# A state-space and FP4 feed-forward kernel: turned xn of group 0 ahead of x of group 1 in the x bank, small VectorE operands in PSUM, group 1 normalised on GpSimd

## The reference

```python
xn = _layernorm(x, axis=-1)
x = x + attn(xn, ...) + ffn(xn, ...)

# attn: per channel a complex recurrence along the sequence, written in the
# reference as an FFT convolution; then times gate = 1 - exp(-decay * scale), real part
phazor = exp((phazor_angle * 1j - decay) * exp(ln_phazor_scale))
y = conv(xn, phazor ** t * phazor_init) + last_conv * phazor ** (t + 1)

# ffn: every operand is quantised to FP4 (E2M1) in blocks of 16, then dequantised
gate, up = q(xn) @ q(w_gate).T, q(xn) @ q(w_up).T       # 128 -> 352
h = silu(gate) * up
out = q(h) @ q(w_down).T                                # 352 -> 128
# q: scale = max(|block|) / 6, rounds |value / scale| to 0, 0.5, 1, 1.5, 2, 3, 4, 6, times scale
```

## Time and profile before

| | us |
|---|---|
| median of 3 runs | 121.84 |
| lowest, highest | 121.81, 121.91 |
| profiled execution, whole | 121.87 |
| its span in the profile | 119.9 |
| busy in it: TensorE | 112.0 |
| VectorE | 102.8 |
| ScalarE | 100.9 |
| GpSimd | 99.7 |

### The profile page before, as it was taken

How to read it: one execution, slowest core, us unless ns; L and a number is a source line. 1 busy time by engine, 2 the same in 40 slices (tenths; PEclk the granted TensorE clock), 3 DMA queues, 4 the chain that set the end, 5 groups by cost and what they waited for, 6 DMA issues and landing times.

```text
span 119.9 us, 2356 instructions
## 1 busy us (share of the span) xinstructions
PE 112.0 (93%) x665; PEld 82.2 (69%) x666; DVE 102.8 (86%) x218; ACT 100.9 (84%) x221; POOL 99.7 (83%) x125
## 2 busy tenths in 40 slices
PE   6999798767999999999999999999999999999992
PEld 2643555234668687767797878688777977989791
DVE  0899999999499999999997999799969999999400
ACT  5759999699997999996899989978997759688950
POOL 4662087989999999999999999999899999999200
PEclk9999999999999999999999999999999999999999
DMA  3992000000000000020002000200002002011112
GB/s 111 322 353 106 3 0 0 3 3 0 5 0 0 0 0 5 0 87 0 0 0 96 0 0 3 87 0 0 5 0 87 0 0 87 5 46 41 53 59 66
DMA packets 3324, 4.90 MB, mean 41 GB/s; under 512 B 497, under 2 KB 1393, under 8 KB 3313
## 3 DMA queue, kind: packets, MB, share of 16 engines
q1 hardware_dynamic: 3168, 4.77, 11.3%
q10 hardware_dynamic: 144, 0.00, 0.1%
HBM read 2.67 MB, written 2.10 MB: 40 GB/s over the span
## 4 chain that ended last, share of the span: by engine, by line
PE 73%; POOL 8%; ACT 6%; DVE 4%; DMA 3%; issue 2%; SPq 1%; POOLq 0%; DVEq 0%; ACTq 0%
PE ps_o L1324 17%; PE ps_g L1248 15%; PE ps_u L1263 14%; PE ps_h L1282 9%; PE ps_u L1270 6%; DMA w_raw<-w_in 3%; PE ps_x L1208 3%; PE ps_o L1310 3%; PE ps_x L1231 3%; POOL vec L468 2%; PE ps_o L1313 2%; DVE ps_u L1632 1%; ACT xbig L840 1%; ACT xsq L833 1%; ACT xq_T L854 1%
## 5 line engine op out<-in xcount | busy, mean ns | idle before, releaser
L1248 PE MATMUL ps_g<-wg_T,xq_T 128*128 128x352 f32 x64 | 24.8, 468 | 1.2 <-ACT xq_T L854 0.7
L1324 PEld LDWEIGHTS ps_o<-wd_T,hq_T 128*128 128x128 f32 x174 | 21.6, 192 | 2.3 <-issue 1.0
L1324 PE MATMUL ps_o<-wd_T,hq_T 128*128 128x128 f32 x174 | 23.1, 276 | 0.0
L1263 PE MATMUL ps_u<-wu_T,xq_T 128*128 128x352 f32 x64 | 22.2, 464 | 0.0
L867 ACT COPY hq_T<-ps_h 128x384 f32<-128x384 f32 x32 | 15.3, 478 | 5.0 <-PE ps_h L1282 4.9
L1686 DVE TENSOR_TENSOR ps_u<-silu,ps_u 128x704 f32<-128x704 f32 (+1 forms) x17 | 14.3, 844 | 2.2 <-PE ps_u L1263 2.1
L861 ACT ACTIVATE silu<-ps_g 128x352 f32<-128x352 f32 x32 | 14.8, 464 | 1.6 <-PE ps_g L1248 1.5
L1282 PE MATMUL ps_h<-ident,hq 128*128 128x128 f32 x96 | 15.9, 274 | 0.3 <-ACT hq_T L867 0.2
L1282 PEld LDWEIGHTS ps_h<-ident,hq 128*128 128x128 f32 x96 | 11.7, 142 | 5.6 <-issue 4.1
L1768 DVE TENSOR_TENSOR ps_u<-ps_u,inv 128x704 f32<-128x704 f32 (+1 forms) x17 | 14.4, 850 | 0.3
L1692 DVE TENSOR_REDUCE ps_u<-ps_u 128x44 f32<-128x704 f32 (+1 forms) x17 | 14.4, 852 | 0.2
(11 more groups left out here) (182 smaller groups left out, 252.2 us busy)
## 6 DMA issues: line engine op xcount, KB each, us to landing
x_all<-x_in SPq DMA_DIRECT2D x8, 256.0 KB, 4.7
out<-x_all SPq DMA_DIRECT2D x7, 256.0 KB, 2.0
w_raw<-w_in SPq DMA_DIRECT2D x2, 192.0 KB, 3.8
out<-x_all SPq DMA_DIRECT2D x4, 64.0 KB, 1.5
w_raw<-w_in SPq DMA_DIRECT2D x1, 176.0 KB, 3.9
par<-params_in ACTq DMA_DIRECT2D x1, 3.5 KB, 2.9
```

The source lines that it names most:

```text
L1248: pe.matmul(ps_g[:, 0:I], x_cols(t), wg_T[:, :], start=True, stop=True).then_inc(s_gate, 1)
L1263: pe.matmul(slot(q)[:, j, 0:I], x_cols(t), wu_T[:, :], start=True, stop=True).then_inc(s_up, 1)
L1324: m = pe.matmul(out_cols(t), hq_T[t % NHT][:, c * P:(c + 1) * P], wd_T[:, c, :], start=False, stop=(c == NCH - 1), skip_group_check=True)
```

## The change

- `turn_xn(0)` now waits only for the first half of group 0's copied x, `turn_xq(1, 1)` for the copy of turned xn of group 0; the bank's alternation is xn 0, x 1, xn 1, x 2 as far as group 2, where it was x 1, xn 0, x 2.
- Narrow VectorE operands move from SBUF to unused columns of PSUM banks: weight maxima, the reciprocals of the gate and up weights, maxima and reciprocals of group 0, maxima of groups 1 and 2, half the reciprocal deviation. The reciprocals of w_down get an instruction and a semaphore of their own (`down_inverses`).
- Group 1 is normalised on GpSimd.
- All lists are in a new order. A second way to compute the statistics of groups 2 to 7, on GpSimd, is added but switched off (`STAT_POOL = False`).

The core of the diff; the lists are cut to the opening, and what is left out there are moves by a few places.

```diff
-    XN_ACT = (0, 1, 2, 3)
+    XN_ACT = (0, 2, 3)
+    STAT_POOL = False
+    XN_FIRST = True
...
+        def weight_inverse(n):
+            return slot(1)[:, n, NCH * P:NCH * P + NCH * P // BLK]
+        def weight_row(n):
+            a = NCH * P + NCH * P // BLK
+            return slot(1)[:, n, a:a + (NCH * P // BLK, WB - NCH * P // BLK)[n]]
+        half_rs = slot(0)[:, 1, 508:508 + TG]
+        def first_row(n, k):
+            a = (XBG // 2) * k
+            return ps_o[:, a:a + XBG // 2] if n else ps_x[:, GT // 2 + a:GT // 2 + a + XBG // 2]
+        def x_row(g):
+            return slot(g - 1)[:, 1, I:I + XBG]
+        def wait_x_bank(eng, g):
+            if g == 1:
+                eng.wait_ge(*((s_xnTc, 1) if XN_FIRST else (s_xqTc, 1)))
+            elif g == 2 and XN_FIRST:
+                eng.wait_ge(s_xqTc, x_done(1))
+            elif g >= 2:
+                eng.wait_ge(s_xnTc, g - 1)
...
# GpSimd's list
             angle_step()
-            decay_step(0)
             theta_step()
             whole_and_part()
+            part_turns()
+            decay_step(0)
             decay_step(1)
+            divide_down()
             decay_step(2)
...
-            part_turns()
-            divide_down()
+            decay_step(7)
+            normalise(1, 0)
+            normalise(1, 1)
             shift_down()
-            decay_step(7)
+            normalise(1, 2)
+            normalise(1, 3)
             shift_back_down()
+            decay_step(8)
             scale_down()
...
+            decay_step(16)
+            divide_x(1)
             first_state(0)
...
# ScalarE's list
             square_x(0, 0)
             square_x(0, 1)
             big_x(0, 0)
+            big_down()
             big_x(0, 1)
-            normalise(1, 0)
-            normalise(1, 1)
             copy_weight(0)
-            big_down()
+            normalise(0, 0)
...
             silu_tile(2)
-            copy_weight(2)
-            out_table(0)
             square_x(1, 1)
             big_x(1, 1)
+            copy_xnT(0)
+            copy_weight(2)
             silu_tile(3)
             copy_in_table(0)
             square_h(0)
             big_h(0)
             normalise(2, 0)
             normalise(2, 1)
             normalise(2, 2)
+            copy_xqT(1, 1)
             normalise(2, 3)
             normalise(3, 0)
-            copy_xqT(1, 1)
+            normalise(3, 1)
+            normalise(3, 2)
+            normalise(3, 3)
+            silu_tile(4)
+            copy_in_table(1)
             square_h(1)
+            silu_tile(5)
             big_h(1)
...
# TensorE's list
             gate_tile(0)
             up_tile(0)
+            up_tile(1)
+            turn_xq(0, 1)
             gate_tile(1)
-            up_tile(1)
             up_tile(2)
             up_tile(3)
             gate_tile(2)
             turn_weight(2)
+            turn_xn(0)
             gate_tile(3)
             in_table(0)
             in_table(1)
+            turn_xq(1, 1)
             round_h(0)
-            turn_xq(1, 1)
             gate_tile(4)
+            turn_h(0)
             up_tile(4)
-            turn_xn(0)
+            up_tile(5)
+            gate_tile(5)
+            gate_tile(6)
             round_h(1)
+            turn_h(1)
+            gate_tile(7)
             up_tile(6)
             up_tile(7)
...
# VectorE's list
+            weight_scales(0)
+            weight_scales(1)
+            stat_guess(0)
             weight_inverses(0)
+            stat_newton(0, 0, 0)
+            down_inverses()
+            weight_inverses(1)
+            stat_newton(0, 0, 1)
+            divide_weight(0)
+            stat_newton(0, 0, 2)
+            divide_weight(1)
             first_maxima(0)
...
+            scan_re(0, 2)
+            product(2)
+            maxima_x(3)
             scale_h(1)
```

More of the change, by code:

```diff
@@ L646, in _ @@
             normalise(5, 2)
+            demodulate_re(0)
             normalise(5, 3)
             divide_x(2)
-            demodulate_re(0)
+            normalise(6, 0)
+            normalise(6, 1)
             demodulate_im(0)
@@ L1010, in _ @@
             copy_hT(5)
-            copy_xqT(3, 1)
+            copy_out(0)
             silu_tile(11)
+            open_out(1)
+            copy_xnT(2)
+            square_h(4)
+            copy_hT(6)
+            big_h(4)
             square_x(4, 1)
-            square_h(4)
-            big_h(4)
+            silu_tile(12)
             big_x(4, 1)
-            silu_tile(12)
             copy_codes(4)
-            copy_out(0)
-            open_out(1)
-            copy_hT(6)
+            copy_hT(7)
@@ L1398, in _ @@
             up_tile(13)
-            sum_down(4)
-            turn_h(7)
             gate_tile(14)
-            sum_down(5)
-            sum_down(6)
-            round_h(5)
-            gate_tile(15)
             turn_h(8)
-            turn_xq(4, 1)
-            up_tile(14)
-            turn_h(9)
-            turn_xn(3)
-            up_tile(15)
-            gate_tile(16)
-            sum_down(7)
-            round_h(6)
             sum_parts(4)
             sum_parts(5)
-            turn_h(10)
+            gate_tile(15)
+            round_h(5)
             sum_parts(6)
             sum_parts(7)
+            turn_xq(4, 1)
+            turn_h(9)
+            sum_down(7)
+            gate_tile(16)
+            up_tile(14)
+            up_tile(15)
+            round_h(6)
+            turn_xn(3)
             gate_tile(17)
@@ L1474, in _ @@
             turn_h(19)
-            turn_xq(7, 1)
+            turn_xn(6)
             up_tile(26)
             up_tile(27)
-            sum_down(16)
-            turn_xn(6)
-            gate_tile(28)
-            sum_down(17)
             sum_down(18)
             turn_h(20)
+            gate_tile(28)
+            sum_down(19)
             turn_xn(7)
-            gate_tile(29)
+            turn_h(21)
             round_h(12)
@@ L1866, in _ @@
             divide_x(0, 1)
+            stat_shift(0)
+            moments(8)
             half_rstd()
-            stat_shift(0)
             scale_weight(0)
+            first_rescale()
             scale_weight(1)
-            first_rescale()
+            scale_x(0, 0)
+            moments(9)
             moments(10)
             moments(11)
-            scale_x(0, 0)
             scale_x(0, 1)
@@ L1892, in _ @@
             moments(28)
+            inverses_x(1)
+            product(0)
             moments(29)
@@ L1938, in _ @@
             divide_h(2)
-            scan_re(0, 3)
+            product(3)
             scan_im(0, 3)
-            product(3)
+            maxima_h(3)
             scale_h(2)
-            maxima_h(3)
             scales(3)
@@ L1946, in _ @@
             divide_h(3)
+            maxima_x(4)
             product(4)
-            maxima_x(4)
             maxima_h(4)
             scales(4)
+            scale_h(3)
             inverses(4)
-            scale_h(3)
+            scan_im(1, 4)
             divide_h(4)
-            scan_im(1, 5)
             product(5)
+            scan_re(1, 5)
             maxima_h(5)
+            scan_im(2, 5)
             scales(5)
@@ L2016, in _ @@
             inverses(13)
-            scan_im(6, 13)
+            scan_re(6, 13)
             divide_h(13)
             product(14)
+            scan_re(7, 14)
             maxima_h(14)
+            scale_h(13)
+            scales(14)
             scan_im(7, 14)
-            scan_re(7, 14)
-            scales(14)
-            scale_h(13)
             inverses(14)
+            product(15)
             divide_h(14)
-            product(15)
             product(16)
```

540 lines of the change are left out of this document (278 added, 262 removed).

## The result

The changed kernel takes 119.95 us (median of 5 runs, 119.48 to 120.07) where the kernel before took 121.81 (121.77 to 121.91) beside it: 1.86 us less by the medians. A second measurement with the same kernel gave 120.15 (119.78 to 120.32), ratio 0.986 [0.984, 0.988]. The forecast was 120.2 with a range of 118.9 to 122.0. The profiled execution took 119.95 us with a span of 118.0; before it was 121.87 with 119.9.

The account below looks back on a forecast made before the run. No engine could be emptied much; the gain lay in the loose opening ahead of 30 us, until all engines run full. Span 119.9 less 1.6, plus 1.97 less 0.03, gave 120.24, called 120.2 us; range 118.9 to 122.0.

Parts of the forecast that it names:

- What bounds it: Whole kernel: no engine can be emptied much; the gain lies ahead of 30 us, with GpSimd's 4.51 us wait at shift_down.
- VectorE's opening: VectorE's first steps: second weight divide at 9.0 instead of 9.99 us, divide_x(0, 0) at 10.95 instead of 11.53.
- ScalarE and GpSimd: Opening: shift_down near 12.95 instead of 14.97 us, divide_x(1) 19.45 instead of 21.70, scale_x(1) ending 25.65 instead of 27.70.
- The hold of a decay step: GpSimd's six L468 steps: one was held some 0.4 us, not expected again; if it returned, divide_x(1) at 19.9.
- The bank swap: TensorE's x bank: second table at 23.6 instead of 24.96 us, gate_tile(4) near 27.15 instead of 29.08.
- What gives some back: TensorE after gate_tile(4): lead down to 0.7 to 1.2 us by 35, 1.2 to 1.9 by 38; 1.6 taken.
- The stops I named: TensorE standing about 0.3 us before turn_h(0), 1.1 before gate_tile(6) and 0.3 before turn_h(1).
- the PSUM operands: VectorE: second weight divide 0.34 us shorter, bounds 0 and 0.34; narrow instructions charged nothing, 0.16 either way in all.
- PSUM operands would cost VectorE more: Rival, ten narrow instructions ahead of divide_x(0, 0): x divides 1.0 us later, gain shrinks to 0.6, 121.2 us; chance 0.04.
- lost in the middle: Rival: 0.7 us of lead left at 35 us never grows, VectorE doing one scan earlier; near 121.1 us; chance 0.18.
- The slower case: Rival, VectorE's scan_re(0, 2): without slack, late demodulate_re(0) delays scale_h(1) and up_tile(6); 0.8 us slower, 122.6; chance 0.15.

Follow-up runs that it names:

- the first experiment: The kernel before with only big_down on ScalarE moved from behind copy_weight(0) to in front of big_x(0, 1): 121.41 us, ratio 0.998.
- the SBUF variant: The changed kernel with all narrow VectorE operands back in SBUF, same lists and waits: 122.88 us, ratio 1.005 to the kernel before.
- `x_row` alone in SBUF: The changed kernel with only the maxima of x of groups 1 and 2 back in SBUF: 121.17 us, ratio 0.995 to the kernel before.

## Why the prediction was right, step by step

*What bounds it.* Right: the four engines' busy times hardly moved, and the gain was made ahead of 30 us. But the 4.51 us at `shift_down`, which I put first, were not the cause by themselves. Mended alone they gave 0.2 to 0.5 and could have given 0.8; put back alone they took 2.0. The same holds for the other parts: undone one at a time they cost about 2.0 (`big_down`), 1.7, or 2.7 with the clock (operands), 0.9 (group 1) and 0.5 to 0.8 (bank order), over 5 us together for a gain of 1.9. They are links of one chain, and whichever is late holds the others. The new order of the lists beyond these parts was not undone by itself, so its own share is not shown.

*VectorE's opening.* Second weight divide forecast 9.0, measured 9.05; `divide_x(0, 0)` 10.95 and 10.96 (the terms given for it add up to 10.89). That they agree to some hundredths here and in the next lines is partly luck: the weights landed 0.18 us later in this trace than in that of before, on which the forecast was built. Counted from the landing, the opening was 0.1 to 0.2 us sooner than forecast. I gave no number for the first gate tile. It brings 0.93 of the 2.1 us, and in the three runs with the opening's narrow operands in SBUF only 0.3, 0.1 and nothing of that is left.

*ScalarE and GpSimd.* `big_down`'s end 12.9 and 12.90, `shift_down` 12.95 and 12.98, `divide_x(1)` 19.45 and 19.24, `scale_x(1)`'s end 25.65 and 25.27; counted from the landing, `divide_x(1)` was 0.4 us sooner than forecast. The hold of a decay step that I did not expect again did not come back in its row (2.06), but a one-column step at 20.74 took 0.53 where its neighbours take 0.19; nothing waited for it. Beside both held steps VectorE ran the same four narrow statistics instructions, which read `bn` from SBUF, at 19.72 to 20.37 us before and at 20.69 to 21.22 after; that these held the steps is likely, but no run tests it.

*The bank swap.* Second table 23.6 and 23.38, `gate_tile(4)` 27.15 and 26.65.

*What gives some back.* The stops I named are there: TensorE's gap before `gate_tile(6)` is 1.04 us by the starts of its matmuls, 1.1 forecast (the row's 0.88 counts from the modelled end), 0.28 before `turn_h(1)`, 0.3 forecast, and 0.2 by the starts before `turn_h(0)`, 0.3 forecast. The lead falls to 0.8 (0.7 to 1.2 forecast) and comes back to 1.5 at 37 (1.2 to 1.9). What is kept is 1.9 by TensorE's work instead of 1.6, and 2.1 counted from the landing of the weights; the difference of 0.3 to 0.5 is about the size of the two gains of 0.2 and 0.5 us by which `divide_x(1)` and `gate_tile(4)` were sooner than forecast. I have no run that ties it to them.

*The term that was mis-sized: the PSUM operands.* I charged 0.34 us for the second divide at most and nothing for the narrow ones. The divide gave 0.52 (1.07 against 0.55), and in the new order one narrow instruction gave 1.26 (1.39 against 0.13). My total came out right for a reason that I had not seen: I took all durations as in the trace of before, and the PSUM operands are what keeps them so once the order has brought `scales_x(2)` next to `demodulate_re(0)`. In the opening they also spare the two `weight_scales` a hold of 0.1 to 0.4 us. In the trace of before the same step, from SBUF, ran beside a row of GpSimd's `normalise`, some 0.43 us a tile, and was not held, as VectorE's and GpSimd's timelines there show:

```profile
29.42 0.20 DVE L1675 TENSOR_SCALAR den_x<-den_x 128x32 f32<-128x32 f32 x1
```

```profile
27.69 3.02 POOL L505 TENSOR_SCALAR xn<-x_all,rstd,shift 128x128 f32<-128x128 f32 x7
```

The rows on which I leaned were of this kind; they could not show the price of meeting a long two-input instruction. Another row of that trace could have: `weight_scales(1)` at 8.02, shown with the first experiment, took 0.29 us, until 0.04 after GpSimd's instruction. Why the short one did not hold `scales_x(2)`, no run here shows.

The Trainium skill ("SBUF — State Buffer", Who interferes with whom) covers this: it frees a VectorE instruction with a single SBUF input from GpSimd only outside the modes that use both ports, says that `tensor_scalar` can take such a mode, and that the blocked side waits for the whole instruction. The runs agree on the length: 1.39 us, to the end of GpSimd's 1.27. Which side waits can't be read from the starts of the rows, since VectorE's begins 0.08 us ahead and it is VectorE that waits. The rule of the Trainium skill's "Perfetto Trace Analysis" (Optimizing Scalar/DVE Operations), by which PSUM operands would cost VectorE more, is not borne out: the narrow groups took 685, 195 and 150 ns from or into PSUM and 696 and 200 with SBUF alone.

*The rivals.* The lead was not lost in the middle. The slower case named the right place (VectorE's row from `divide_h(1)` to `scan_re(0, 2)`, with no slack), and in the SBUF variant the kernel was indeed slower through it, but by a held VectorE instruction rather than by a late `demodulate_re(0)`.

## What to carry to other kernels

The largest wait in a trace is not the largest gain: ask what else ends within a microsecond of it, and expect little before all of these are moved. When a reorder puts a VectorE instruction that reads and writes SBUF beside a long GpSimd instruction, price it at the rest of that instruction, not at its own length, and ask who is queued behind it. A TensorE stop of some 2 us can cost the stop and then the clock, so a variant may be slower by more than its delay.

## What the runs showed of the hardware

A VectorE instruction of 32 columns from SBUF to SBUF, 0.13 us with its input in PSUM, took 1.39 us when it began 0.08 us ahead of a GpSimd instruction of 1.27 us, and ended 0.04 us after it; it did so at 29.20 in one variant, at 28.70 in another and at 29.18 in a third. An instruction of 46 columns from SBUF to SBUF took 0.80 us when it began 0.52 us behind a GpSimd instruction of 1.27 us, and 0.29 when it began 1.02 behind; both times it ended 0.04 us after it. Two narrow inputs in SBUF are held too: in the run with `big_down` back the first instruction on `bn` (24 columns), beside `divide_x(1)` on GpSimd, took 1.03 us, where it takes 0.20 in the changed kernel.

After stops of TensorE of 2.04 and 2.05 us the granted clock was at 0.50 to 0.70 of 2.4 GHz over two stretches of 2 us in two profiles, and stayed at 1.00 in a third with the same 2.05; after the 1.73 of the earlier trace rows and the 0.88 of the changed kernel it stayed at 1.00. Where it fell behind the late silu, it cost some 0.6 us with `x_row` alone in SBUF and 1.1 to 1.4 with everything there. What decides between the two after equal stops, no run here shows.

The landing of the weight transfer, from 6.3 to 7.1 us, moves the whole kernel with it, unless something else in the opening ends later: TensorE's row of idle matmuls, which took 5.99 to 6.84 us, as in the run with the old bank order, or a held `weight_scales`. That is as large as several of the effects measured here.
